# Rows turned inside expert blocks, job banks for wide batches, a later projection in tanh attention

## The reference, cut to what matters

```
x = x + L0 attention (focused linear attention over the context)
x = x + L0 experts   (top 2 of 8, gated: silu(g) * u, capacity 560 rows per expert, 256 -> 2 x 1024 -> 256)
x = x + L1 attention (16 heads of 16; softmax(tanh(q k^T * scale) * exp(log_C) with masked keys) v W_out^T)
x = x + L1 shared experts with LoRA
x = x + L2 attention (16 heads of 64: the "wide" one; q, k, v projections, softmax, output * tanh(gate))
x = x + L2 experts   (top 2 of 8, gelu, no capacity limit)
x = x + L3 attention (16 heads of 16, masked softmax)
x = x + L3 ternary feed-forward with a convolution
```

## Time and profile before

| | us |
|---|---|
| median of 3 runs | 3054.76 (3051.03 to 3055.73) |
| profiled execution | 3083.54 |
| its span, first to last instruction | 3081.8 |
| mean granted TensorE clock | 0.928 |
| busy: PE / DVE / ACT / POOL | 2581.3 / 1374.2 / 1121.8 / 824.1 |

### The profile page before, as it was taken

How to read it: one execution, slowest core, us unless ns; L and a number is a source line. 1 busy time by engine, 2 the same in 40 slices (tenths; PEclk the granted TensorE clock), 3 DMA queues, 4 the chain that set the end, 5 groups by cost and what they waited for, 6 DMA issues and landing times. The chain is left out here.

```text
span 3081.8 us, 47764 instructions
## 1 busy us (share of the span) xinstructions
PE 2581.3 (84%) x15928; PEld 1781.0 (58%) x15928; DVE 1374.2 (45%) x4831; ACT 1121.8 (36%) x2609; POOL 824.1 (27%) x878
## 2 busy tenths in 40 slices
PE   6998859999938878979999999984999559999586
PEld 4776437777714434547766555663888436666344
DVE  6987502222133444336643333430111357777665
ACT  4554311111118970114444333331333126666321
POOL 3443030000042210007754344503000401212442
PEclk8999879999979998979999999997999769999798
DMA  4232362222022110034210000035777410000000
GB/s 134 84 116 78 146 204 85 84 86 74 14 95 78 60 42 24 0 93 144 111 45 7 11 6 6 1 123 195 293 285 289 140 34 11 10 8 6 28 7 18
DMA packets 69923, 252.33 MB, mean 82 GB/s; under 512 B 16395, under 2 KB 32040, under 8 KB 52264
## 3 DMA queue, kind: packets, MB, share of 16 engines
q1 hardware_dynamic: 60008, 226.24, 20.9%
q0 software_dynamic: 9744, 23.87, 2.5%
HBM read 197.97 MB, written 52.10 MB: 81 GB/s over the span
## 5 line engine op out<-in xcount | busy, mean ns | idle before, releaser
L2597 PE MATMUL L_ffne_up<-L_ffne_xT,L_ffne_wu 128*128 128x128 f32 (+1 forms) x2144 | 391.5, 340 | 33.2 <-DVE L_ffne_xT L2521 23.3
L2597 PEld LDWEIGHTS L_ffne_up<-L_ffne_xT,L_ffne_wu 128*128 128x128 f32 x2144 | 332.2, 194 | 92.9 <-ACT L_ffne_hT L2508 27.5
L1349 PEld LDWEIGHTS L_xattn_pt<-ident,L_xattn_p 112*125 112x125 f32 x1536 | 207.3, 189 | 183.4 <-issue 77.5
L1044 POOL TENSOR_SCALAR L_xattn_p<-L_xattn_p,L_xattn_rec 112x375 f32<-112x375 f32 x256 | 311.6, 1225 | 0.0
L1349 PE MATMUL L_xattn_pt<-ident,L_xattn_p 112*125 112x112 f32 x1536 | 257.7, 289 | 20.9 <-DVE L_xattn_pt L1203 16.0
L1203 DVE COPY L_xattn_pt<-L_xattn_pt 125x336 f32<-125x336 f32 x448 | 216.9, 499 | 125.6 <-PE L_xattn_pt L1349 125.5
L2583 PE MATMUL L_ffne_dn<-L_ffne_wd,L_ffne_hT 128*112 128x256 f32 (+1 forms) x1200 | 266.2, 379 | 1.5 <-issue 1.5
L1186 DVE TENSOR_REDUCE L_xattn_least<-L_xattn_s 112x1 f32<-112x375 f32 x256 | 128.4, 543 | 250.7 <-PE L_xattn_s L1337 250.5
L2583 PEld LDWEIGHTS L_ffne_dn<-L_ffne_wd,L_ffne_hT 128*112 128x112 f32 (+1 forms) x1200 | 216.9, 183 | 39.7 <-issue 2.1
L2484 POOL DMA_DIRECT2D L_ffn_ybuf<-L_ffne_y x75 | 40.1, 534 | 689.1 <-DVE L_ffne_y L2536 405.6
L1127 ACT ACTIVATE L_xattn_p<-L_xattn_ssb,L_xattn_least 112x375 f32<-112x375 f32 x256 | 153.8, 602 | 129.9 <-DVE L_xattn_least L1192 129.0
(11 more groups left out here) (357 smaller groups left out, 4602.2 us busy)
## 6 DMA issues: line engine op xcount, KB each, us to landing
L_ffne_wd<-in_L_ffn_down SPq DMA_DIRECT2D x43, 1024.0 KB, 4.8
L_ffne_wu<-in_L_ffn_up SPq DMA_DIRECT2D x35, 1024.0 KB, 5.4
L_ffne_wu<-in_L_ffn_up SPq DMA_DIRECT2D x8, 2048.0 KB, 7.9
L_xattn_kt<-L_xattn_kd SPq DMA_DIRECT2D x8, 1500.0 KB, 7.7
L_xattn_v<-L_xattn_vd SPq DMA_DIRECT2D x8, 1500.0 KB
L_ffn_xbuf<-L_ffnr_zeros SPq DMA_DIRECT2D x8, 1120.0 KB, 11.8
fa_ctxT<-in_ctxT SPq DMA_DIRECT2D x16, 375.0 KB, 3.6
fa_rows<-in_ctx_rows SPq DMA_DIRECT2D x16, 375.0 KB
```

Source lines behind the costliest of these rows:

```text
L1044: p = pool.tensor_scalar(p_sb[:, head % RP, :], p_sb[:, head % RP, :], rec[:, h, head:head + 1], None, ALU.mult)
L1349: m = pe.transpose(pt_ps[head % 2][0:KP, 0, kt * S:(kt + 1) * S], p_sb[:, head % RP, kt * KP:(kt + 1) * KP], ident[0:S, 0:S])
L2597: m = pe.matmul(up_ps[s % RING][k][:, 0, 0:RH], wu[:, h, c, k * FF + f * 128:k * FF + (f + 1) * 128], xT[:, h, c, q * RH:(q + 1) * RH], st ...
```

## The change: what it does

Four edits.

1. In `run_experts` the rows of block b+1 are turned and copied within block b: a tile after each of the steps 6, 8, 10, 12 and 14 of a gated block, the one tile after step 4 of an ungated block.
2. In `tanh_attention` TensorE projects batch b-2 in batch b, behind `transpose_x(b+1)` and ahead of `scores 2`; VectorE does the residual of b-2 ahead of `take_o(b-1)`. The batch loops of TensorE and VectorE are written out; those of the other engines stay.
3. In wide attention one pool `free_ps` of four banks holds scores and jobs. Turns 0 to 6 use three for scores and one for jobs; turns 7 to 15 use two for scores and two in turn for jobs, by a plan made when the program is built (`plan`, `wait_bank`). The slots of k and v jobs change; those of q, y and x keep their heads.
4. In turns 7 to 15 of wide attention, both `turn_p` of a pair stand together, then the jobs of both slots, then the products.

```diff
                 def body(b, h):            # tanh attention, VectorE
-                    if not isinstance(b, int) or b < NB - 1:
+                    if b < NB - 1:
                         normalize(b + 1, 1 - h)
                         take_xt(b + 1, 1 - h)
-                    if not isinstance(b, int) or b > 0:
-                        ch = Chain(dve, chain, (b - 1) * PER)
+                    ch = Chain(dve, chain, max(0, (b - 2) * PER + 1))
+                    if b > 1:
+                        residual(b - 2, h, ch)
+                    if b > 0:
                         take_o(b - 1, 1 - h)
                         divide(b - 1, ch)
-                        residual(b - 1, 1 - h, ch)
...
                     if not last:           # tanh attention, TensorE
                         transpose_x(b + 1, 1 - h)
+                    if b > 1:
+                        project(b - 2)
                     scores(b, h, 2)
...
                     products(b, h, 0)
-                    if not first:
-                        project(b - 1)
...
     if wide:
-        slots = [[K[0]], [K[1]], [K[2]], [K[3]], [K[4]], [K[5]], [K[6]], [K[7]], [Q[0]], [Q[1], V[0]],
-                 [Y], [V[1], V[2]], [V[3]], [V[4]], [V[5]], [X]]
+        slots = [[K[0]], [K[1]], [K[2]], [K[3]], [K[4]], [K[5], K[6]], [K[7]], [], [Q[0]], [Q[1]], [Y],
+                 [V[0]], [V[1], V[2]], [V[3]], [V[4], V[5]], [X]]
+        slots_loaded = [[], [], [], [], [], [], [], [], [Q[0]], [Q[1]], [Y], [], [], [], [], [X]]
...
-    NS, NJ = (3, 1) if wide else (4, 1)
+    FREE = 4 if wide else 5
+    SWITCH = FROM - 1 if wide else NB
+
+    def score_banks(b):
+
+        return 2 if wide and b >= SWITCH else FREE - 1
...
+        def plan(kind, i, turn, b, h):
+
+            first = 2 if wide and turn >= SWITCH else FREE - 1
+            spare = range(first, FREE)
+            at = spare[planned[first] % len(spare)]
+            planned[first] += 1
+            bank_of[kind, i, b] = at
+            if at in last_user:
+                bank_free[kind, i, b] = last_user[at]
+            elif at < FREE - 1:
+                bank_free[kind, i, b] = ("score", SWITCH * H - 1, 0)
+            last_user[at] = (kind, b, i)
...
-                    after(pe, exp_done if wide else low_done, b * H + pair + 2 - NS)
+                    after(pe, exp_done if wide else low_done, b * H + pair + 2 - score_banks(b))
...
                     for pair in range(0, H, 2):      # wide attention, TensorE
                         scores(b, h, pair)
+                        together = wide and b >= SWITCH
                         trail(b, h, pair, LT, turn_p)
+                        if together:
+                            trail(b, h, pair + 1, LT, turn_p)
                         slot_jobs(job, b, h, pair, "kqvxyz")
-                        trail(b, h, pair + 1, LT, turn_p)
+                        if together:
+                            slot_jobs(job, b, h, pair + 1, "kqvxyz")
+                        else:
+                            trail(b, h, pair + 1, LT, turn_p)
                         if (pair - LP) % SIDE == 0:
                             trail(b, h, pair, LP, products)
-                        slot_jobs(job, b, h, pair + 1, "kqvxyz")
+                        if not together:
+                            slot_jobs(job, b, h, pair + 1, "kqvxyz")
...
+        TURN_AT = {(6 + 2 * t if gated else 4): t for t in range(NT)}   # experts
...
                         if s == 1 and not first(b):
                             second(b - 1, 1 - h)
-                    if not last(b):
-                        turn_rows(b + 1, 1 - h)
+                        if s in TURN_AT and not last(b):
+                            turn_rows(b + 1, 1 - h, TURN_AT[s])
```

More of the change, by code:

```diff
@@ L802, in body @@
                     products(b, h, 0)
-                    if not first:
-                        project(b - 1)
                 transpose_x(0, 0)
                 pe.wait_ge(w_in, NLOADS * 16)
-                each_batch(pe, body)
+                for b in range(NB):
+                    body(b, b % 2)
+                project(NB - 2)
                 products(NB - 1, 1, 1)
@@ L900, in softmax_attention @@
         onT = sb("onT", [128, OC, S])
-        job_ps = [core.banks(ctx, f"{n_}job{i}", 1) for i in range(NJ)]
-        s_ps = [core.banks(ctx, f"{n_}s{i}", 1) for i in range(NS)]
+        free_ps = [core.banks(ctx, f"{n_}s{i}", 1) for i in range(FREE)]
         pt_ps = [core.banks(ctx, f"{n_}pt{i}", 1) for i in range(2)]
@@ L971, in projections, with jobs_at @@
                 run("x", 0, -1, 1, 1)
+        def jobs_at(b, head):
+            return (slots_loaded if wide and b < SWITCH else slots)[head]
         def slot_jobs(run, b, h, head, kinds):
-            for kind, i in slots[head]:
+            for kind, i in (jobs_at(b, head) if wide else slots[head]):
                 of = b + OF[kind]
@@ L977, in slot_jobs, with job_bank, wait_bank @@
                     run(kind, i, b, of, (h + OF[kind]) % 2)
+        bank_of, bank_free = {}, {}
+        def plan(kind, i, turn, b, h):
[9 more added lines that the diff above has]
+            last_user[at] = (kind, b, i)
+        planned, last_user = {2: 0, FREE - 1: 0}, {}
+        projections(plan)
+        for turn in range(NB):
+            for head in range(H):
+                slot_jobs(plan, turn, turn % 2, head, "kqvxyz")
+        if not wide:
+            plan("z", 0, NB, NB - 1, 1)
+        plan("y", 0, NB, NB - 1, 1)
+        def job_bank(kind, i, b):
+            return free_ps[bank_of[kind, i, b] if wide else FREE - 1]
+        def wait_bank(pe, kind, i, b):
+            if (kind, i, b) in bank_free:
+                was, of, n = bank_free[kind, i, b]
+                if was == "score":
+                    pe.wait_ge(exp_done, of + 1)
+                else:
+                    pe.wait_ge(done[was], made(was, of, n))
         with nc.Block() as block:
@@ L1273, in job @@
                 def job(kind, i, turn, b, h):
-                    wait_bank(pe, kind, i, turn)
-                    ps = job_ps[order.index((kind, i)) % NJ]
+                    wait_bank(pe, kind, i, b)
+                    ps = job_bank(kind, i, b)
                     if kind == "k":
@@ L1336, in scores @@
                             q, k = qbd[r, h, n // HG, n % HG // 2, :], keys.kt[r, b, n // HG, :]
-                        m = pe.matmul(s_ps[bank(b, n)][0:S, 0, 0:SK], q, k, start=True, stop=True)
+                        m = pe.matmul(score_ps(b, n)[0:S, 0, 0:SK], q, k, start=True, stop=True)
                     m.then_inc(s_out, 2)
@@ L2547, in body @@
                     if first(b):
-                        take_rows(0, 0)
+                        for t in range(NT):
+                            take_rows(0, 0, t)
                     for s in range(UPB):
@@ L2588, in body @@
                     if first(b):
-                        turn_rows(0, 0)
+                        for t in range(NT):
+                            turn_rows(0, 0, t)
                     pe.wait_ge(up_in[h], (b - h) * 8 + 16)
```

83 lines of the change are left out of this document (34 added, 49 removed).

## The result

| | before | changed |
|---|---|---|
| median, us | 3052.9 (3049.52 to 3055.73, 4 runs) | 2971.49 (2970.09 to 2974.75, 4 runs) |
| profiled execution, us | 3083.54 | 2970.94 |
| span, us | 3081.8 | 2969.2 |
| mean granted TensorE clock | 0.928 | 0.932 |

The ratio is 0.9735, 95% interval 0.9718 to 0.9752: 81.4 us faster.

A forecast was written before the change was run, and what follows sets the result against it. It took TensorE's idle time as what can be won, with ScalarE the floor in tanh attention. Gains of 23.8 + 10.7 + 14 + 16 = 64.5 us gave 3054.8 - 64.5 x 0.99 = 2991 us, range 2975 to 3014.

The forecast's parts named there:

- A turn with other work behind it advances by 0.34 (a turn of 112 rows); I take 0.35 for 128: L2 experts: assumed TensorE cost in us of a moved turn, leaving 0.72 us saved per turn, 23.8 us over 33.
- for 35 entries into and out of short turns: L0 experts: 0.7 us given back from 11.4 us of waits, leaving 10.7 us.
- All 1.58 go: Wide attention, turns 7 to 14: two job banks remove all 1.58 us a batch of v job waits.
- tight points: Tanh attention: TensorE's score starts fit with 0.2 us to spare, VectorE's residual before `take_o` with some 0.3 us.
- Priced at nothing: Tanh attention: written-out loops need instructions fetched by DMA, whose share there is 0.17; counted as no cost.
- 1.58 + 1.26 - 1.0: Wide attention, us per batch: job waits removed, plus new order's gain, less new exp waits; 1.8 in all.
- minus 2: Wide attention, turn 15: without k or v jobs, seven pairs lose up to 0.4 us each, partly given back.
- L2 bound by DMA: Rival, L2 experts: blocks become DMA-bound and stay at 8.18 us, time 3015 us; chance 0.06.
- Clock falling in turns 7 to 15: Rival, wide attention: new waits draw TensorE's clock to 1.2 GHz, about 3200 us if throughout; chance 0.02.
- Wide attention giving nothing: Rival: waits for exp take what the second job bank gives, time 3007 us; chance 0.10.
- tanh attention keeping its pace: Rival: `take_o` behind the residual, or fetched instructions, cancel the gain there, time 3005 us; chance 0.12.
- The offset: Whole kernel: profiled execution's 28.8 us above the median carried over, with 0.99 on the gain: 3054.8 - 64.5 x 0.99.

The follow-up runs named there:

- by its run alone: Kernel before with one function of the changed one: run_experts 3035.61 us, tanh_attention 3068.43, softmax_attention 3068.54; the column gives the change in its stages.
- e7: Changed kernel with each turn of rows within the expert blocks issued twice (the first block's once); 3012.91 us, ratio 0.9770.
- e10: Changed kernel with the L2 experts' rows turned behind step 6 of a block, not step 4; 2985.64 us, ratio 0.9773.
- e5: Changed kernel with wide attention's old order restored; two score banks, two job banks and new slots kept; 3000.28 us, ratio 0.9729.
- e11: Changed kernel with tanh attention's old order, the loops of TensorE and VectorE still written out; 2979.79 us, ratio 0.9759.
- e6: Changed kernel with one job bank and three score banks in all turns, new slots and order kept; 3057.21 us, ratio 0.9916.
- e3: Kernel before with only the changed tanh_attention; 3068.43 us, ratio 0.9951.
- e9: Changed kernel once more, no edit, on another chip where the kernel before takes 3053.5 us; 2969.04 us, ratio 0.9719.
- e8: Changed kernel with ScalarE's copies of K7 and V5 in wide attention put behind the second head's exp; 2991.93 us, ratio 0.9690.
- e1: Kernel before, profiled once more with no edit; 3086.09 us.

## Why the prediction was right or wrong

All four gains came, where I had said: from the copies of turned rows, from scores in tanh attention and from v jobs in wide attention. Their sizes were too small, in every term, and the high bounds with them. In wide attention one of the numbers that came true did so by luck.

| term | said (bounds) | by its run alone | before to after | mean of all traces |
|---|---|---|---|---|
| L2 experts | 23.8 (20 to 24) | 30.4 | 28.3 | 29.5 |
| L0 experts | 10.7 (9 to 11.4) | 16.8 | 19.9 | 18.4 |
| tanh attention | 14 (8 to 14.9) | 18.1 | 16.2 | 15.8 |
| wide attention | 16 (5 to 20) | 19.9 | 20.6 | 19.5 |
| sum | 64.5 | 85.2 | 85.0 | 83.2 |

The last column is the mean over every trace that has a stage's old code less the mean over those that have its new code; it evens out the some us by which a stage differs from trace to trace.

**The failed step is "A turn with other work behind it advances by 0.34 (a turn of 112 rows); I take 0.35 for 128"**, and with it the idle time of a wait taken for all that the wait costs. The turn advances by 0.22 and 0.19 (after), 0.22 and 0.20 (e7). The row that I took it from is a turn ahead of scores, matmuls over 64 rows. It is the scores that the 0.34 goes with, and not the wait of 0.56 us ahead of the turn: in wide attention of the kernel before, a turn of the same size ahead of such scores advances by 0.34 with no wait at all.

```profile
1616.76 0.41 PE L1300 MATMUL L_xattn_job<-ident,L_xattn_xn 112*128 112x112 f32 x2
1617.10 0.89 PE L1337 MATMUL L_xattn_s<-L_xattn_kt,L_xattn_qt 64*112 64x375 f32 x4
```

In L2 the step left 1.07 - 0.35 = 0.72 a block. Right were 1.07 - 0.22 = 0.85 and 0.10 for the slower steps behind the wait, which I had at nothing: 0.95, and the blocks show 0.94. Over 33 blocks the first error is 4.3 us and the second 3.3. In L0 I took 0.7 us off "for 35 entries into and out of short turns", where the blocks show 0.71 us a block to be added: 7 x (1.65 + 0.71) = 16.5 us. The rest, up to 18.4 or 19.9, is mostly the stretches at the 1.2 GHz level, which I had left out altogether.

All three terms with waits of TensorE have one root, which e10 measured by itself: a wait cost more than its idle time. In L2 that gives 33 x (0.69 + 0.24) = 30.7, in L0 7 x (1.65 + 3 x 0.24) = 16.6. In wide attention "All 1.58 go" was right as to the waits, but 2.2 us a turn went with them (e5), some 5 us over eight turns. Together these make 7.6 us in L2, 6 in L0 and 5 in wide attention, about the 16.9 us that the sum of 64.5 lacks of the measured 81.4. I took the idle time for the whole, and the upper bounds of both expert terms (24 and 11.4) were made in that way too, so the truth lay beyond them.

**Tanh attention.** Floor and tight points held: 11.51 us a batch where I had 11.62, ScalarE without waits. "Priced at nothing" for the written-out loops failed, in the good direction: they carry 0.58 of 1.26 us a batch (e11). That doesn't change the sum, as the floor is ScalarE's either way; it changes the reason for nearly half of it, so the size is right in part by luck.

**Wide attention.** A turn fell by 2.2 (banks and slots) + 1.41 (order) - 0.95 (exp waits) = 2.66 us, where I had added up 1.58 + 1.26 - 1.0 and then taken 2.2. That the order gave about the 1.26 that I had is luck. I had put all of it down to large jobs that no longer stand ahead of scores, 7 x (1.46 - 1.28). But ahead of products a k job advances by 1.37, so only half of that came, about 0.6 to 0.7 us. The other half is the two `turn_p` of a pair standing together, 8 x (0.83 - 0.74) = 0.7, which the prediction's 1.26 doesn't have. The Trainium skill's rule (TensorE: Matmul & The Clock Gate, What happens when you issue a matmul), by which weights are pulled ahead of running matmuls where row groups don't conflict, I had read as giving the whole 1.26; the trace agrees with the direction and not with that size. The page's other case, a kernel in which PSUM double-buffering gave no further gain (HAM oscillation), is not this one: with the new order and no second job bank the stage is 60.7 us longer (e6). Turn 15 waits 3.0 us for the exp in all, against 0.6 before; I had put minus 2 there.

**The rivals.** L2 bound by DMA: no; the DMA share rose to 0.89 at 326 GB/s, more than the 0.84 that I had, and PE waits 0.2 us for it in 31 blocks. Clock falling in turns 7 to 15: no, 1.00 up to 1918 us. The "about 3200" that I gave for that case was mis-added: nine turns of some 48 us at half the clock would add about 430 us, not 210. Wide attention giving nothing, tanh attention keeping its pace: no.

**The offset.** That the profiled execution stood 28.8 us above the median I carried over as it was, which is what the runs bear out: 75.5 + 112.1 - 57.8 - 101.5 = 28.3 us of it are the combine stages on one chip against the other. Only the factor 0.99 on the gain had no ground.

## What to carry to other kernels

Moving a short turn into the midst of other matmuls wins more than the idle time that the trace shows, here some 0.24 us more for each wait in the expert stages: compare times from start to start with and without the wait, and price a moved TensorE instruction by a row that has the same kind of matmul behind it as the new place. A second PSUM bank for jobs is worth most where jobs come in pairs, but look then at which copies stand ahead of an exp in ScalarE's queue; here moving two entries of a table gave 7 us more. Look also where within a stage the granted clock falls: here such stretches went when the waits went. And compare profiles from the same chip only, stage by stage, untouched stages too.

## What the hardware showed that I had not expected

- **VectorE held up by GpSimd.** In tanh attention the same tensor_scalar (L101, 112x256) takes 0.29 us in all batches of before; of after, from 925 us on, it takes 1.02 to 1.03 eleven times and 0.89 twice. In the rows above it starts at 983.24, within GpSimd's product for `ta_qbd` (982.29 to 984.12), and ends 0.14 us behind it. In the last three batches, with no such product beside it, it takes 0.29 again. The new order has put the two side by side. e3 and e9 show the same, and e11, with the old order, takes 0.29 to 0.30 throughout. The Trainium skill (SBUF — State Buffer, SBUF: two separate sides) has a port pair that VectorE and GpSimd lock for a whole instruction; this trace agrees with it. It cost nothing here: `take_o` behind it still waits 0.26 us for TensorE's products. But of a margin that would have been 0.26 + 0.74 = 1.0 us it took 0.74.
- **A hardware loop costs even within its body.** 0.67 us over the edge and 0.29 inside it, against 0.07 written out, between two dependent instructions of VectorE (e11). Written out, the instructions also have fixed addresses where the loop computes them; no run separates the two.
- **A wait costs 0.24 us beside its idle time** in the expert stages, for waits of 0.24, of 0.69 and of 0.55 us in the mean (e10, and before against after); 0.26 for the job waits of e6, and 0.07 for the exp waits that e8 took away.
- **What follows a short turn sets its price.** A turn of 112 rows advances by 0.19 us ahead of the L0 up matmuls (565.11 to 565.30), 0.25 ahead of the projection (980.13 to 980.38), 0.34 ahead of scores over 64 rows, with and without a wait in front (1112.56 in the earlier trace rows, 1616.76).
- **Short falls of the clock in a busy stage.** Six short stretches at the 1.2 GHz level in the L0 experts of four traces, each worth some 1.6 us, each 3.0 to 3.3 us behind the start of a block's row of turns with its waits; none in ten traces without those waits. That the waits bring them on is argued from this count and not shown by a run of its own.
- **Idle stretches of TensorE that go with the chip (or the hour).** 57 and 101 us against 75 and 111 in two stages whose code is the same, with gaps of 3 to 7 us that no semaphore in the trace ends (e1, e8, e9).
